# Causal row maximum of two of four score banks by a reversed running maximum on VectorE, in a fused cross-attention and mixture-of-experts kernel

## The reference, cut to what matters

```
x = x + xattn(layernorm(x), ctx_512, Wq, Wkv_expand, Wout)      # x: 8 x 128 x 256, ctx: 8 x 128 x 64
x = x + ffn(layernorm(x), router and 8 experts with LoRA, top 2)

# xattn: 16 heads of 16 features
scores = einsum('bhqd,bhkd->bhqk', qh, kh) / sqrt(16)
scores = where(tril(ones(sq, sk)), scores, finfo.min)            # causal: key <= query
attn   = softmax(scores, axis=-1)
out    = einsum('bhqk,bhkd->bhqd', attn, vh) ... @ Wout.T
```

## Time and profile before

| what | value |
|---|---|
| median of 3 runs | 170.72 us |
| the profiled execution, its own time | 170.58 us |
| its span, first to last instruction | 168.8 us |
| busy: PE, PEld, DVE, ACT, POOL | 153.3, 118.9, 105.4, 80.1, 53.5 us |
| mean granted TensorE clock | 0.998 |
| the chain that ended last, by engine | PE 65%, DVE 14%, DMA 8%, ACT 5% |
| mask products, line 894 | 9.6 us in 32, TensorE |
| row maxima, line 593 | 20.4 us in 32, VectorE |

### The profile page before, as it was taken

How to read it: one execution, slowest core, us unless ns; L and a number is a source line. 1 busy time by engine, 2 the same in 40 slices (tenths; PEclk the granted TensorE clock), 3 DMA queues, 4 the chain that set the end, 5 groups by cost and what they waited for, 6 DMA issues and landing times.

```text
span 168.8 us, 3777 instructions
## 1 busy us (share of the span) xinstructions
PE 153.3 (91%) x1481; PEld 118.9 (70%) x1481; DVE 105.4 (62%) x224; ACT 80.1 (47%) x161; POOL 53.5 (32%) x93
## 2 busy tenths in 40 slices
PE   0597999999999999999999997999969989999972
PEld 0365676677777677778778876887758868888961
DVE  2778986859657657835498456555943466444463
ACT  1373557356657776586754617422653022222420
POOL 4276002256378657776740243330000000000000
PEclk9999999999999999999999999999999999999999
DMA  5999940000000000000000185000000594000003
GB/s 148 292 255 229 282 126 2 6 6 0 8 0 8 0 6 2 4 2 4 0 0 4 37 257 209 0 4 0 2 0 4 144 344 137 0 0 0 4 0 124
DMA packets 13042, 11.18 MB, mean 66 GB/s; under 512 B 6457, under 2 KB 10449, under 8 KB 13025
## 3 DMA queue, kind: packets, MB, share of 16 engines
q1 hardware_dynamic: 9584, 7.14, 15.7%
q0 software_dynamic: 544, 2.10, 4.6%
q10 hardware_dynamic: 2896, 1.70, 3.9%
HBM read 9.79 MB, written 1.08 MB: 64 GB/s over the span
## 4 chain that ended last, share of the span: by engine, by line
PE 65%; DVE 14%; DMA 8%; ACT 5%; issue 5%; POOL 1%; DVEq 0%; ACTq 0%
PE bank L798 29%; PE bank L1087 9%; PE bank L908 8%; DMA probsT<-weights 4%; PE bank L894 4%; PE bank L1024 4%; PE bank L915 3%; DVE m_sb L593 2%; DVE h_f L671 2%; DMA x_sb<-in_x 2%; DMA weights<-wT 2%; DVE xhat L552 2%; PE bank L973 2%; ACT silu L410 1%; DVE stats L539 1%
## 5 line engine op out<-in xcount | busy, mean ns | idle before, releaser
L798 PE MATMUL bank<-xT_hi,up_hi 128*128 128x512 f32 x64 | 27.1, 424 | 3.0 <-ACT silu L410 3.0
L318 ACT ACTIVATE h_hi<-h_f 128x512 fp32r<-128x512 f32 x16 | 10.1, 632 | 37.2 <-PE bank L1087 25.9
L295 POOL TENSOR_SCALAR_AFFINE_SELECT probsT<-probsT 128x512 f32<-128x512 f32 x32 | 19.7, 635 | 22.5 <-ACT probsT L391 22.5
L593 DVE TENSOR_REDUCE m_sb<-bank 128x4 f32<-128x512 f32 x32 | 20.4, 685 | 9.4 <-PE bank L908 9.4
L391 ACT ACTIVATE probsT<-bank 128x512 f32<-128x512 f32 x32 | 17.9, 590 | 17.3 <-PE bank L915 17.3
L798 PE MATMUL bank<-xT_hi,up_lo 128*128 128x512 f32 x64 | 25.3, 395 | 0.0
L798 PE MATMUL bank<-xT_lo,up_hi 128*128 128x512 f32 x64 | 25.3, 395 | 0.0
L676 DVE TENSOR_TENSOR h_lo<-h_f,h_hi 128x512 fp32r<-128x512 f32 x16 | 11.4, 713 | 21.0 <-ACT h_hi L318 21.0
L1087 PE MATMUL bank<-dn_hi,h_hi 128*128 128x256 f32 x64 | 18.4, 288 | 1.1 <-DVE h_lo L676 1.0
L915 PE MATMUL bank<-q_f,k_f 32*128 32x128 f32 x256 | 18.6, 283 | 0.0
L798 PEld LDWEIGHTS bank<-xT_hi,up_hi 128*128 128x128 f32 x64 | 12.0, 188 | 8.6 <-ACT silu L410 6.9
(11 more groups left out here) (137 smaller groups left out, 284.4 us busy)
## 6 DMA issues: line engine op xcount, KB each, us to landing
probsT<-weights SPq DMA_DIRECT2D x16, 256.0 KB, 5.5
x_sb<-in_x SPq DMA_DIRECT2D x4, 256.0 KB, 4.8
up_w<-in_L_ffn_gate_up_proj ACTq DMA_DIRECT2D x1, 1024.0 KB, 10.4
up_w<-in_L_ffn_gate_up_proj POOLq DMA_DIRECT2D x1, 1024.0 KB, 7.2
dn_w<-in_L_ffn_down_proj POOLq DMA_DIRECT2D x1, 1024.0 KB, 9.3
out<-x_sb SPq DMA_DIRECT2D x4, 256.0 KB, 2.2
ctx_sb<-in_ctx ACTq DMA_DIRECT2D x2, 128.0 KB, 5.6
wq_raw<-in_L_xattn_Wq ACTq DMA_DIRECT2D x1, 256.0 KB, 5.8
```

What stands on the lines that cost most here:

```text
L295: pool.affine_select(out=ch, in_=ch, compare_op=ALU.is_ge, fill=0.0, base=0, pattern=[[0, 4], [1, P]], channel_multiplier=-1).then_inc(S_( ...
L318: act.activation(out_, in_, ACT.Copy, scale=scale).then_inc(S_(done), 1)
L593: dve.reduce_max(m_sb[:, b % 2, :].rearrange("p (u j t) -> p j u t", u=2, t=2)[:, c], S_BANK(b, c)[:, :].rearrange("p (u t n) -> p u t n", ...
L798: last = pe.matmul(out_, a, m, start=start and i == 0, stop=stop and i == len(pairs) - 1, **kw)
```

## The change

Groups 0 and 1 of every batch get no mask product; their score products start the bank themselves. VectorE takes their maximum with `tensor_tensor_scan` over the 512 columns from the last to the first: state = max(state + resets, score). `resets` is 0 except at key = query in each head, where it is -2^127, so that the state forgets the keys behind the query; column 0 of each head then holds the causal maximum. The scan writes all 512 columns, so `m_sb` becomes 128 x 4 x 4 x 128 with one buffer, and `max_chunk(b, 0)` waits for `max_T(b - 1)`. Groups 2 and 3 keep mask and reduction. The maxima are no longer negated by VectorE but by the copy to `mT`. The heads are numbered anew, so that the 16 maxima stand in the order of group and head; the copies to `q_f` and `k_f`, `load_max`, `values` and the softmax division follow, and the division's multiply becomes two instructions. GpSimd makes `resets` right after `causal`. `equal` moves into space that is free later, to make room.

```diff
+    SCANNED = (0, 1)
...
+        resets = sb("resets", [P, 4 * P], BF16)
...
-        m_sb = sb("m_sb", [P, 2, NH])
+        m_sb = sb("m_sb", [P, NC, 4, P])
...
-                    sp.dma_start(q_f[HD * (1 - u):P:32, 2 * u:2 * u + 2, tokens(b)], mT[u * NH // 2:(u + 1) * NH // 2, :])\
+                    sp.dma_start(q_f[HD * (1 - u):P:32, u:NC:2, tokens(b)], mT[u:NH:2, :])\
                         .then_inc(m_loaded[b % 2], 16)
...
+            link(pool.memset(resets[:, :], 0.0))
+
+            diagonals = resets[:, :].rearrange("p (h n) -> p h n", h=4)
+            pool.affine_select(out=diagonals, in_=diagonals, compare_op=ALU.not_equal, fill=MASKED, base=0,
+                               pattern=[[0, 4], [-1, P]], channel_multiplier=1).then_inc(S_("resets_made"), 1)
             pool.dma_start(up_w[:, 1, :, :], gate_up.rearrange("e (c p) o -> c p e o", p=P)[1]).then_inc(ld["up1"], 16)
...
-                copy(mT[:, :], M_BANK(b), "mT_copied")
+                copy(mT[:, :], M_BANK(b), "mT_copied", -1.0)
...
             def max_chunk(b, c):
                 dve.wait_ge(S_("s_ready"), NC * b + c + 1)
-                if b >= 2 and c == 0:
-                    dve.wait_ge(S_("mT_ready"), b - 1)
-                dve.reduce_max(m_sb[:, b % 2, :].rearrange("p (u j t) -> p j u t", u=2, t=2)[:, c],
-                               S_BANK(b, c)[:, :].rearrange("p (u t n) -> p u t n", u=2, t=2), AX.X, negate=True)\
-                    .then_inc(S_("max_done"), 1)
+                if b == 0 and c == 0:
+                    dve.wait_ge(S_("resets_made"), 1)
+                if b and c == 0:
+                    dve.wait_ge(S_("mT_ready"), b)
+                if c in SCANNED:
+                    dve.tensor_tensor_scan(m_sb[:, c, :, :].rearrange("p h n -> p (h n)")[:, ::-1], resets[:, ::-1],
+                                           S_BANK(b, c)[:, ::-1], MASKED, ALU.add, ALU.max).then_inc(S_("max_done"), 1)
+                else:
+                    dve.reduce_max(m_sb[:, c, :, 0], S_BANK(b, c)[:, :].rearrange("p (h n) -> p h n", h=4), AX.X)\
+                        .then_inc(S_("max_done"), 1)
...
-                dve.tensor_tensor(o_heads, on[:, :, :, 0:HD], r_den[:, :, :, None].to_broadcast([P, 2, NH // 2, HD]), ALU.mult)\
-                    .then_inc(S_("o_nat_ready"), 1)
+                for t in range(2):
+                    last = dve.tensor_tensor(o_heads[:, t], on[:, t, :, :, 0:HD],
+                                             r_den[:, t, :, :, None].to_broadcast([P, 2, NH // 4, HD]), ALU.mult)
+                last.then_inc(S_("o_nat_ready"), 1)
...
                         if s:
                             pe.wait_ge(S_("max_done"), n - 3 if s == 1 else n - 1)
-                        pe.matmul(S_BANK(s, j)[:, :], ident_b[:, :], causal[:, :, :].rearrange("p h n -> p (h n)"),
-                                  start=True, stop=True, skip_group_check=True)
+                        if j not in SCANNED:
+                            pe.matmul(S_BANK(s, j)[:, :], ident_b[:, :], causal[:, :, :].rearrange("p h n -> p (h n)"),
+                                      start=True, stop=True, skip_group_check=True)
...
                             last = pe.matmul(S_BANK(s, j)[:, c * P:(c + 1) * P], q_f[rows, c, tokens(s)], k_f[rows, c, tokens(s)],
-                                             start=False, stop=True, skip_group_check=True)
+                                             start=j in SCANNED, stop=True, skip_group_check=True)
...
-                pe.transpose(M_BANK(b), m_sb[:, b % 2, :], ident[:, :]).then_inc(S_("mT_ready"), 1)
+                pe.transpose(M_BANK(b), m_sb[:, :, :, 0].rearrange("p j c -> p (j c)"), ident[:, :]).then_inc(S_("mT_ready"), 1)
```

More of the change, by code:

```diff
@@ L96, in cross_attention_moe_kernel @@
         shift2 = sb("shift2", [P, NT])
-        m_sb = sb("m_sb", [P, 2, NH])
+        m_sb = sb("m_sb", [P, NC, 4, P])
         mT = sb("mT", [NH, P])
         oT_sb = sb("oT_sb", [P, 4, P])
-        r_den = sb("r_den", [P, 2, NH // 2])
+        r_den = sb("r_den", [P, 2, 2, NH // 4])
         o_nat = sb("o_nat", [P, NH, HD])
@@ L107, in cross_attention_moe_kernel @@
         above = sb("above", [P, GT, E, E])
-        equal = sb("equal", [P, GT, E, E])
         earlier = sb("earlier", [P, E, E])
@@ L141, in cross_attention_moe_kernel @@
         h_lo = sb("h_lo", [P, 2, GN], F32R)
-        rest_of_qk = sb("rest_of_qk", [P, 6 * GN])
+        equal = sb("equal", [P, GT, E, E])
+        rest_of_qk = sb("rest_of_qk", [P, 6 * GN - GT * E * E])
         w_dram = nc.dram_tensor("weights", (NG, E, GN), F32, kind="Internal").ap()
@@ L349, in k_copy @@
                 for u in range(2):
-                    spread(k_f[:, 2 * u, pair(p)], K_BANK(p, 0)[:, 0:PN], u, first[:, 1 - u:2 - u], "k_by_act")
+                    spread(k_f[:, u, pair(p)], K_BANK(p, 0)[:, 0:PN], u, first[:, 1 - u:2 - u], "k_by_act")
             def q_copy(p):
@@ L354, in q_copy @@
                 for u in range(2):
-                    spread(q_f[:, 2 * u, pair(p)], Q_BANK(p, 0)[:, 0:PN], u, zero_col[:, :], "q_by_act")
+                    spread(q_f[:, u, pair(p)], Q_BANK(p, 0)[:, 0:PN], u, zero_col[:, :], "q_by_act")
             def values(g):
@@ L568, in k_copy @@
                 for u in range(2):
-                    spread(k_f[:, 2 * u + 1, pair(p)], K_BANK(p, 1)[:, 0:PN], u, first[:, 1 - u:2 - u], "k_by_dve")
+                    spread(k_f[:, 2 + u, pair(p)], K_BANK(p, 1)[:, 0:PN], u, first[:, 1 - u:2 - u], "k_by_dve")
             def q_copy(p):
@@ L573, in q_copy @@
                 for u in range(2):
-                    spread(q_f[:, 2 * u + 1, pair(p)], Q_BANK(p, 1)[:, 0:PN], u, zero_col[:, :], "q_by_dve")
+                    spread(q_f[:, 2 + u, pair(p)], Q_BANK(p, 1)[:, 0:PN], u, zero_col[:, :], "q_by_dve")
             def merge(n):
@@ L599, in x2T_low @@
                 low(xT_lo[:, :, t * P:(t + 1) * P], X2_BANK(t), xT_hi[:, :, t * P:(t + 1) * P], "x2T_lo")
-            on = bank[5][:, :].rearrange("p (u h w) -> p u h w", u=2, w=32)
-            o_heads = o_nat[:, :, :].rearrange("p (h u) d -> p u h d", u=2)
+            on = bank[5][:, :].rearrange("p (t u j w) -> p t u j w", t=2, u=2, w=32)
+            o_heads = o_nat[:, :, :].rearrange("p (t j u) d -> p t u j d", t=2, u=2)
             def softmax_divide(b):
@@ L607, in softmax_divide @@
                     dve.wait_ge(S_("o_T"), b)
-                dve.reciprocal(r_den[:, :, :], on[:, :, :, HD]).then_inc(S_("r_den_ready"), 1)
+                dve.reciprocal(r_den[:, :, :, :], on[:, :, :, :, HD]).then_inc(S_("r_den_ready"), 1)
                 dve.wait_ge(S_("r_den_ready"), b + 1)
-                dve.tensor_tensor(o_heads, on[:, :, :, 0:HD], r_den[:, :, :, None].to_broadcast([P, 2, NH // 2, HD]), ALU.mult)\
-                    .then_inc(S_("o_nat_ready"), 1)
+                for t in range(2):
+                    last = dve.tensor_tensor(o_heads[:, t], on[:, t, :, :, 0:HD],
+                                             r_den[:, t, :, :, None].to_broadcast([P, 2, NH // 4, HD]), ALU.mult)
+                last.then_inc(S_("o_nat_ready"), 1)
             def residual(b):
@@ L1022, in values @@
                     for j in range(4):
-                        h = 8 * (c % 2) + 2 * j + c // 2
+                        h = 8 * (c // 2) + 2 * j + c % 2
                         last = pe.matmul(bank[4][32 * j:32 * j + VW, c * P:(c + 1) * P], v_sb[:, b, h, :],
```

## The result

The changed kernel takes 175.69 us, the median of 4 runs (175.00 to 176.39), beside 170.64 for the kernel before; the ratio is 1.0292 with a 95% interval of 1.0244 to 1.0341. It is slower, as forecast, and inside the range of 170.8 to 177.0, but 1.7 us above the 174.0 forecast. Three things make up what lies above 174.0, in other shares in each execution. The changed order itself costs about 0.6 us more than I had worked out. What lies ahead of the attention came 0.08 us later than before in one profile and 0.60 in another. And two of the four executions had a mean granted TensorE clock of 0.98; in the profiled one of them the clock was at 1.2 GHz for some 7 us.

What follows compares the result with a forecast made beforehand. TensorE (91% busy) bounds most of the kernel, VectorE already paces iteration 2; running delays of 0.50, 0.96, 2.16, 2.72, 3.07 and 3.41 us put 3.4 on the profiled 170.58: 174.0 us, range 170.8 to 177.

Steps and rivals of the forecast that it cites:

- The scan's price: One VectorE scan of 128x512 from PSUM: estimated at 1.21 us, with 0.69 from below and 3.0 from above.
- two slopes: Each scanned element costs VectorE twice the plain per-element time: 163 ns + 512 x 2.04 = 1.21 us; chance 0.74.
- The order of waits: In iterations 3 to 5, second-half scores start at least 0.2 + 2.34 + 0.44 = 2.98 us after the first pair's old start.
- The saving behind a wait: Iteration 0, first half: removed mask product lies behind the maxima's wait; scores at 25.37 instead of 24.87, delay 0.50.
- the divided division: Softmax division's multiply on VectorE becomes two before iteration 2's scans: 0.08 to 0.17 us more, taken as 0.15.
- The new wait: First scan of batch b + 2 waits for TensorE's max_T(b + 1): 0.2 us more.
- resets at no cost: GpSimd's making of resets moves one weight load and one normaliser by 1.2 us, costing nothing; uncovered, 0.2.
- The scan at the price of a reduction: Rival: a scan takes 0.69 us, delaying no second half of iterations 3 to 5; -1.9, 168.7 us; chance 0.15.
- it evens out: Rival: a scan near 0.87 us, or more usable spare VectorE time; 170.6 to 170.8 us; chance 0.05.
- a scan is dearer: Rival: three slopes, 1.73 us a scan, each pair 1.04 longer; +10.7, 181 us; chance 0.06.

## Why the prediction was right, and where it was short

The delays of the scores behind the kernel before, from the profile of the changed kernel without the fallen clock. I take 0.60 us off for its start: the statistics began 0.13 later, and the xhat pair took 0.47 longer. The first profile of the changed kernel had no longer xhat pair and started 0.08 later. Up to the fall of its clock it gives the same delays: scores at 25.70 and 38.31, so 0.75 and 1.35.

| scores start in | before | after - 0.60 | delay | forecast |
|---|---|---|---|---|
| iteration 0, first half | 24.87 | 25.64 | 0.77 | 0.50 |
| iteration 1, second half | 36.88 | 38.25 | 1.37 | 0.96 |
| iteration 2, second half | 44.00 | 46.46 | 2.46 | 2.16 |
| iteration 3, second half | 51.87 | 55.00 | 3.13 | 2.72 |
| iteration 4, second half | 59.35 | 62.90 | 3.55 | 3.07 |
| iteration 5, second half | 66.78 | 70.77 | 3.99 | 3.41 |

**The scan's price** was right: 1.21 us estimated, 1.205 measured, and a scan of half the length fits the two slopes. The reason given for two slopes was an argument and had no row behind it; the nearest row, the reduction's, spoke for 0.69. That the value came out to 5 ns is partly luck.

**The order of waits** was right: the pair of scans, 2.34 us both forecast and measured, and the bank's release decide the second halves, and the delay goes through undiminished to the end (3.99 at the last maxima; the span is 4.6 longer, less 0.60 for the start).

**The saving behind a wait** was mis-sized. I let the scores start 0.05 us after the maxima where no mask product stands between. In the trace there are 0.35 us of issue before the first products of iteration 0 at 26.24. With the mask product back in that place they start 0.44 after the last maximum, so taking it out behind this wait saves 0.09 and not 0.39. This is 0.27 of the delay at iteration 0. What fills the 0.35 isn't shown: TensorE had stood still for 1.0 us there, and the same call also waits for the DMA of the first maxima. It isn't so behind every wait: in iteration 2 of the kernel with six scans the scores start 0.09 after the maximum (43.64 and 43.73).

**Up to iteration 1** another 0.14 is added, which makes the 0.41 there. Of it 0.12 lie in VectorE's stretch from the second pair to the scans, 4.20 us (31.89 to 36.09) where it was 4.08: the merges start only when the LoRA products end, at 33.21. Up to iteration 2 the excess falls again, to 0.30: I had counted 0.15 for the divided division, and from the scores of iteration 1 to the scans it takes 5.45 us instead of 5.39. The first scan of iteration 2 starts 1.43 us later than the reduction did, where 1.1 was forecast.

**The new wait** is the transpose's 0.23 and 0.09 of issue and start, so 0.33 us instead of my 0.2, and on the path in iterations 3 to 5: 0.1 each, 0.28 together. With the 0.30 at iteration 2 this makes the 0.58.

**resets at no cost** holds in half of the profiles; in the other half VectorE's xhat pair, beside the memset, is 0.47 us longer. I had covered GpSimd's queue and not the engine beside it. That it shows in the median time is not shown.

**The clock** was not in the forecast at all. It makes the difference between a median of 175.69 in the first four executions and 175.0 to 175.2 in the two later groups, whose ratio is 1.022; my 174.0 to 170.7 is 1.019. Of the errors in the order of waits 0.69 were too low and 0.11 too high, so little of the agreement comes from errors that cancel.

**The rivals.** The scan at the price of a reduction fell with the durations; but its sum, -1.9, fits the kernel without scan and mask, -1.7 by the medians and -2.0 by the ratio. That it evens out, and that a scan is dearer, fell with the same row.

## What to carry to other kernels

To move work from a full engine to one that is 62% busy, look not at the share but at the distance between the moment the second engine gets its input and the moment the first needs its result; here that was 2.0 to 2.2 us with 1.3 used, and the longer work needed 3. The same exchange placed where the distance is over 3 us made the kernel 0.6% faster. Look at what starts behind the wait before counting a removed instruction at its full length: here the removal of 0.39 us saved 0.09 in one place and 0.35 in another.

## What was not expected of the hardware

A scan of 128x512 costs 1.21 us, backwards or forwards, with addition and maximum or with two maxima, and one of 128x256 0.67, while the addition of two operands of 128x512 costs 0.68. TensorE's granted clock fell to 1.2 GHz from 38.3 to 45.1 us in one profile, after 8-column products and a wait of 0.41 us; from 34 to 38 us TensorE had been busy for 3.41 us. The executions with a mean clock of 0.98 were about 1.2 us above the median of the others. Two VectorE instructions from SBUF to SBUF, the second xhat pair, took 1.38 us beside a GpSimd memset of 0.66 in six profiles and 1.85 beside one of 0.53 in six others; an equal pair at 6.6 to 6.8 us, with nothing of GpSimd beside it, took 0.73. The second pair took 1.38 in the kernel before as well, beside the making of `causal`.
